# Forty-eight more turns of the identity in TensorE's order, at three places of the second half

## The reference

```python
x = x + tanh(g_xattn[0]) * L0_xattn(ctx, layernorm(x))     # 8 heads of 64, keys = context and tokens, 589 keys
x = x + tanh(g_ffn[0])   * L0_ffn(layernorm(x))            # quantised weights and rows, conv over 3 tokens, silu
x = x + tanh(g_xattn[1]) * L1_xattn(layernorm(x), ctx, ctx)# 16 heads of 8, rotary, 77 keys
x = x + tanh(g_ffn[1])   * L1_ffn(layernorm(x))            # 8 experts, the best 2 per token, and a shared one
```

## Time and profile before

| | us |
|---|---|
| median of 3 runs | 272.95 |
| lowest, highest | 271.57, 273.73 |
| the profiled execution, its own time | 269.39 |
| its span, first to last instruction | 267.6 |
| busy in the span: PE, DVE, ACT, POOL | 255.1, 223.9, 190.8, 32.2 |
| mean granted clock of PE, share of full speed | 0.98 |

### The profile page before, as it was taken

The page is one execution under the profiler, slowest core; times in us unless marked ns, Lnnn a source line. Parts: engine busy times, 40 slices in busy tenths (PEclk is TensorE's granted clock), DMA queues, the critical chain, the costliest instruction groups (busy, mean ns, idle before and its releaser), DMA issues.

```text
span 267.6 us, 5491 instructions
## 1 busy us (share of the span) xinstructions
PE 255.1 (95%) x1782; PEld 188.7 (71%) x1782; DVE 223.9 (84%) x551; ACT 190.8 (71%) x474; POOL 32.2 (12%) x57
## 2 busy tenths in 40 slices
PE   7899999999999999999999999979989798999996
PEld 3567778777788876787778887758756554566675
DVE  6599988967578769999996889999999898698861
ACT  1578868786668787698997954577997888645551
POOL 3000101100101001000000112400021201242330
PEclk9999999999999999999999999999999796899999
DMA  6292392301200034003000000000000000000001
GB/s 187 56 246 76 79 312 69 90 2 25 67 1 4 0 90 92 0 0 80 15 2 0 2 0 2 1 1 2 0 1 2 2 2 0 0 2 21 10 13 39
DMA packets 8850, 10.71 MB, mean 40 GB/s; under 512 B 1116, under 2 KB 5878, under 8 KB 8822
## 3 DMA queue, kind: packets, MB, share of 16 engines
q1 hardware_dynamic: 7792, 9.70, 13.5%
q10 hardware_dynamic: 1029, 0.65, 0.8%
HBM read 4.99 MB, written 0.52 MB: 21 GB/s over the span
## 4 chain that ended last, share of the span: by engine, by line
PE 77%; DVE 14%; issue 4%; ACT 4%; DVEq 0%; ACTq 0%
PE slot L532 22%; PE slot L621 13%; PE slot L602 6%; PE slot L603 6%; PE slot L713 3%; PE slot L762 3%; PE slot L696 3%; PE slot L756 3%; PE slot L583 2%; PE slot L768 2%; PE slot L628 2%; PE slot L577 2%; ACT S L923 2%; PE slot L681 2%; PE slot L592 1%
## 5 line engine op out<-in xcount | busy, mean ns | idle before, releaser
L845 ACT ACTIVATE PR<-slot,nm 128x589 f32<-128x589 f32 x64 | 47.7, 750 | 11.5 <-DVE nm L1071 11.0
L1071 DVE TENSOR_REDUCE nm<-slot 128x1 f32<-128x589 f32 x64 | 46.9, 764 | 7.4 <-PE slot L603 6.9
L532 PE MATMUL slot<-K,PR 128*128 128x128 f32 (+1 forms) x320 | 44.7, 277 | 0.5 <-ACT PR L845 0.3
L532 PEld LDWEIGHTS slot<-K,PR 128*128 128x128 f32 (+1 forms) x320 | 35.9, 142 | 11.3 <-issue 5.5
L602 PE MATMUL slot<-KH,Q 128*128 128x296 f32 (+1 forms) x128 | 41.1, 337 | 0.2 <-DVE KL L1065 0.2
L621 PE MATMUL slot<-PT,V 128*64 128x256 f32 (+1 forms) x320 | 38.1, 384 | 0.0
L603 PE MATMUL slot<-KL,Q 128*128 128x296 f32 (+1 forms) x128 | 36.2, 299 | 0.0
L780 ACT ACTIVATE PT<-slot 128x640 f32<-128x640 f32 x45 | 30.7, 704 | 6.4 <-PE slot L532 6.1
L621 PEld LDWEIGHTS slot<-PT,V 128*64 128x64 f32 (+1 forms) x320 | 21.6, 137 | 11.9 <-issue 2.7
L602 PEld LDWEIGHTS slot<-KH,Q 128*128 128x128 f32 x128 | 24.2, 189 | 2.6 <-DVE PT L782 0.7
L603 PEld LDWEIGHTS slot<-KL,Q 128*128 128x128 f32 x128 | 24.2, 189 | 0.7 <-issue 0.5
(11 more groups left out here) (174 smaller groups left out, 510.4 us busy)
## 6 DMA issues: line engine op xcount, KB each, us to landing
KH<-KH SPq DMA_DIRECT2D x16, 147.5 KB, 2.5
KL<-KL SPq DMA_DIRECT2D x16, 147.5 KB, 2.6
CTT<-in_ctxT SPq DMA_DIRECT2D x1, 640.0 KB, 4.9
K<-in_const SPq DMA_DIRECT2D x1, 589.0 KB, 5.7
WGU<-in_wgu SPq DMA_DIRECT2D x1, 580.0 KB, 6.7
out<-X SPq DMA_DIRECT2D x8, 64.0 KB, 1.5
L1W<-in_l1w SPq DMA_DIRECT2D x1, 384.0 KB, 3.6
WD<-in_wdT SPq DMA_DIRECT2D x1, 320.0 KB, 7.3
```

Of the source, the lines that this page charges most:

```text
L532: return pe.transpose(dst, src, ident[0:p, 0:p])
L845: act.activation(PR[:, s, :], W[:, K0:K0 + KEYS0], ACT.Exp, bias=nm0[:, s:s + 1], accum_out=sum0[:, b, p * 2 + f, t, e:e + 1]).then_inc(pr ...
L1071: dve.tensor_reduce(nm0[:, s:s + 1], W[:, K0:K0 + KEYS0], AX.X, ALU.max, negate=True).then_inc(max_ready, 1)
```

## The change

Three words of `PLAN` get turns; nothing else is touched. The plan is read as before, so the bank's former holder follows from the order.

```diff
-... a4:D3 f2:F2 f2:A1 a2:D1 f2:F3 ...
+... a4:D3 f2:F2+17@3 f2:A1 a2:D1 f2:F3 ...
-... a4:D1 f4:D3 a1:F7 a1:P1 a6:D2 a4:A1 a1:A1
+... a4:D1 f4:D3 a1:F7+17@6 a1:P1 a6:D2 a4:A1 a1:A1
-... a4:A1 a6:P1 a4:B a4:Ca a4:B a6:D2 ...
+... a4:A1 a6:P1 a4:B+14@1 a4:Ca a4:B a6:D2 ...
```

More of the change, by code:

```diff
@@ L125 @@
 w:F2 w:A1 f4:D3 n:P2 a3:F0 n:D3 w:D1 o:F2 a3:D1 o:D1 o:F5 a4:F2 o:D1 a4:D1 a4:A1 a4:B a4:F0 a4:Ca a4:A1 a1:F7 a1:A1 n:P2 a4:B+8@4 a4:D1
-a4:F6 n:D3 a2:F5 f1:F4 a4:A1 a4:D1 f1:A1 a4:Ca f1:D1 a4:D3 f2:F2 f2:A1 a2:D1 f2:F3 f2:A1 f2:D1 a4:B a4:Ca f2:A2 f2:D1 f2:F5+3@4 f2:D2 f2:F2+7@4 f2:A1
+a4:F6 n:D3 a2:F5 f1:F4 a4:A1 a4:D1 f1:A1 a4:Ca f1:D1 a4:D3 f2:F2+17@3 f2:A1 a2:D1 f2:F3 f2:A1 f2:D1 a4:B a4:Ca f2:A2 f2:D1 f2:F5+3@4 f2:D2 f2:F2+7@4 f2:A1
 a4:A1 f2:A1 f2:D1 f2:A2 a4:F4+26@0 a4:B f2:D2 f2:D1 f2:A2 a4:Ca a4:F6+8@0 a4:D1 f2:A2 f2:D2 a3:P1 a4:A1 f2:D2 a1:P1 a4:D1 f3:F2 f3:D1 f3:F1+2@0 f3:F3 a4:A1
@@ L129 @@
 f3:A1 a1:P1 f4:A1 f4:D2 f4:P2 a4:D1 f4:B+6@1 a1:P1 a6:D0 f4:D3 a4:F4 a6:P1 f3:Ca a4:A1 f4:F7 a1:F1 f4:D2 a6:F6 a4:D1 a1:A1 a2:F0 a4:D3 a4:B a6:A1
-a6:D1 f4:A1 a4:A1 f4:B a4:B a4:Ca a2:D1 f4:D2 a4:F2 a4:D1 a4:F0 f4:P2 a4:Ca a4:A1 a4:D3 a6:B a4:F4 a4:D1 f4:D3 a1:F7 a1:P1 a6:D2 a4:A1 a1:A1
+a6:D1 f4:A1 a4:A1 f4:B a4:B a4:Ca a2:D1 f4:D2 a4:F2 a4:D1 a4:F0 f4:P2 a4:Ca a4:A1 a4:D3 a6:B a4:F4 a4:D1 f4:D3 a1:F7+17@6 a1:P1 a6:D2 a4:A1 a1:A1
 a4:B a4:Ca a4:D1 a4:B a6:D0 a4:Ca a4:F6 a2:F2 a4:D3 a4:D1 a6:P1 a4:A1 a6:P2 a6:F1 a4:B a6:D3 a4:A1 a4:B a6:A1 m1:F0 a4:Ca m1:A1 a2:D1 a4:D3
-a6:D1 a4:F4 a4:F2 m3:F0 a4:D1 a4:Ca a4:D1 a6:B a6:D0 a4:F6 a4:A1 a4:A1 a6:P1 a4:B a4:Ca a4:B a6:D2 m3:D1 a4:Ca m3:A1 a4:D1 a4:A1 a4:F4 m3:D2
+a6:D1 a4:F4 a4:F2 m3:F0 a4:D1 a4:Ca a4:D1 a6:B a6:D0 a4:F6 a4:A1 a4:A1 a6:P1 a4:B+14@1 a4:Ca a4:B a6:D2 m3:D1 a4:Ca m3:A1 a4:D1 a4:A1 a4:F4 m3:D2
 a6:F2 a6:P2 a6:A1 m2:F0 a4:D1 a6:D1 m2:A1 a6:D3 a4:B m2:B a4:A1 m1:F3 a4:D3 a4:Ca a4:D3 m2:A2 a6:B a4:B a6:D0 m2:F6 m2:P1 m2:D1 a4:Ca m2:B
```

## The result

The changed kernel takes 273.39 us, the median of 20 runs, against 271.84 us of the kernel before in the same runs: a ratio of 1.0059, 95% interval 1.003 to 1.0088. It is 1.6 us slower. The forecast was 0.6 us slower with a range of 270.4 to 277.2; the time lies in it, and the direction was right. The profiled execution took 272.25 us with a span of 270.5, where the one before had 269.39 and 267.6: 2.9 us more. The two figures differ because executions of one and the same kernel differ in how long PE's clock is down, and because the ten products with which PE starts (L768) take 6.0 us in one trace and 7.6 in another. The profiled execution before had a mean clock of 0.980; in the 57 executions of the kernel before that were timed beside the experiments the mean was 0.973 (0.961 to 0.987), in 19 of the changed kernel 0.989 (a twentieth, of 294.1 us at 0.844, is left out of this mean).

The account below looks back on a forecast made before the run. PE was taken as busy nearly everywhere, with DVE setting the pace from 176 to 209.7 us and half-speed stretches after PE's idle gaps. 1.06 + 2.2 - 2.6 = +0.6 us on 272.95 gave 273.6 us, range 270.4 to 277.2.

Parts of the forecast that it names:

- the sum of +0.6: Whole kernel: 1.06 + 2.2 - 2.6 us over the three places, carried onto 272.95 to give 273.6 us.
- First place: 17 turns in bank 3 ahead of `f2`: PE 1.32 us late, DVE starts 1.06 us late; cost 1.06 us.
- hangs on what PE does around a gap: Argument that the clock fell behind the second gap but not the equally long first; for full clock at both places.
- faster rival: Timed runs lose two more half-speed stretches, one behind the first place: -2.8 us, 270.1 us; chance 0.12.
- Second place: 17 turns in bank 6 ahead of `a1`: PE idle until L1270 ends, then turns; cost 2.2 us, ends 0.97 and 3.9.
- in this trace the clock is 0.50 until 212.5: Second place: 1.19 us worth of full-speed work from 210.13 to 212.5, turns end at 213.2; cost 2.2 us.
- Third place: 14 turns in bank 1 ahead of `a4`: 0.56 us late, but full clock behind them; gain 2.6 us.
- that cover is enough: Third place: PE waits 0.4 us for ACT's L930, but three other words precede `m1`'s turns; supports the 2.6 us gain.
- the 3.56 us: Timed runs' excess over the profiled 269.39 us, carried over; guessed as more half-speed stretches, two with 1.7 us each.
- slower rival: Clock falls behind the third place in spite of the turns: +4.3 us, 277.2 us; chance 0.28.
- Full clock at both places: Rival: PE keeps full clock at second and third places, second costing 0.97: -0.6 us, 272.4 us; chance 0.15.

Follow-up runs that it names:

- kernel with one turn: Kernel before with only one turn in bank 6 at the second place, in place of seventeen: 273.93 us, ratio 1.0113.
- the fitted kernel: Kernel before plus 4 turns in bank 3, 17 in bank 7, 4 in bank 1 at the three places: 266.61 and 266.31 us, ratios 0.9839 and 0.9833.

## Why the prediction was right, and which terms were off

The time lay in the range and the direction held, but two of the three terms were off, and that the forecast of 273.6 us came within 0.2 of the 273.39 measured is luck: the sum of +0.6 was 1.0 us too low against the timed runs (2.3 too low against the traces), and the base, the median of three runs at 272.95, lay 1.1 us above the 271.84 of twenty. One reading of the rows was off without weight: below full speed are three of the slices between 207 and 234 us, not four.

**First place: right in mechanism and size.** Forecast 1.06 us of delay of DVE; measured 1.12 in the changed kernel (1.23 at L1122 less the 0.11 of lag) and 1.1 in the kernel with this edit alone. What I did not see is that the clock falls behind this gap in other executions. I had inferred from one trace that it "hangs on what PE does around a gap"; but in the kernel with the third place alone all is unchanged up to here and the clock in 176 to 189 us is 0.87, where it was 1.00. There the gap costs 1.3 us: L681 behind the 26 turns stands at 188.04, less 1.45 us of start lag 186.59, against 185.28 before. Seventeen turns spare this in some executions and cost 1.1 in all; four spare it and cost nothing. This was part of my faster rival, which the one trace spoke against; it exists, but is worth only 1.3 us in some executions, not 3.4.

**Second place: right in mechanism, undersized.** Forecast 2.2 us with ends of 0.97 and 3.9; measured 3.93 - 1.22 = 2.7. PE waited for L1270 as forecast, 0.57 us longer than before (2.45 against 1.88). The step that was off is "in this trace the clock is 0.50 until 212.5": the sum left the half-speed stretch where it had been, so that most of it fell on idle time and on turns that nobody waits for. It came some 3 us later, from about 212.4 us on. The seventeen turns took 2.48 us up to the work behind them, where they took 1.95 at full clock in bank 7, and the real work from there to L681 took 2.51 in place of 1.52. The kernel with one turn shows that the seventeen turns aren't needed for the cost.

**Third place: the term that was off most.** Forecast a gain of 2.6 us if the clock holds; it held, and the gain was 3.93 - 2.87 = 1.06. The time from the start of L681 ahead of the place to the start of L751 behind it tells the two parts of this term apart:

| kernel | turns at the third place | clock behind it | L681 to L751, us |
|---|---|---|---|
| before | none | 0.50 | 11.92 |
| 17 in bank 7 at the second place alone | none | 1.00 | 9.87 |
| 4 at the third place alone, and the fitted kernel | 4 | 1.00 | 9.87 |
| changed | 14 | 1.00 | 10.86 |

So fourteen turns delay by 0.99 us, where the sum had 0.56: the turns of `S` start 1.05 us late (226.69 less 3.93 is 222.76, before 221.71), and L681 behind them then waits 0.25 us for ACT's copy L794, a wait that the prediction didn't have. And full clock gives back only 2.05 us, where the sum had 3.17, half of the half-speed stretch. This larger part is lost even where no turn delays anything.

The failed step is "that cover is enough". I set only ACT's L930 against PE, and not DVE's L1008 behind it. Five turns of `S` behind L713 PE is still 1.98 us ahead of its former course in the changed kernel (231.67 less 3.93, against 229.72), and 2.98 where nothing is delayed (7.32 us from L681, against 10.30). Two words later it waits 0.64 us for the rows `XN` that L1008 normalises, in every one of these traces with full clock. The lines of the kernel with 17 turns in bank 7 alone:
```profile
220.06 0.79 PE L681 MATMUL slot<-KBD,Q 32*128 32x308 f32 x4
...
227.38 0.71 PE L532 MATMUL slot<-K,S 128*128 128x128 f32 x5
...
228.30 1.40 DVE L1008 TENSOR_SCALAR XN<-X,mvx,vex 128x128 f32<-128x128 f32 x2
228.32 1.04 POOL L520 TENSOR_TENSOR HM<-HM,cwt 128x512 f32<-128x512 f32 x1 [4.79 <-ACT HM L946]
...
229.59 0.50 PE L532 MATMUL slot<-K,XN 128*128 128x128 f32 x2 [0.64 <-ACT PT L794]
229.93 0.61 PE L751 MATMUL slot<-L1W,A1T 128*128 128x128 f32 x4
```

The profile names L794 as the releaser here. But the turns read what L1008 writes, and they begin 0.14 us after the first of the two L1008 ends, which took 1.15 us; before, at 209.55, that distance was 0.14 as well. In the changed kernel it is the same, by the line's least, median and greatest duration in ns and POOL's timeline:
```profile
L1008 DVE TENSOR_SCALAR XN<-X,mvx,vex x2: 332/762/1191, 232.5 to 233.7; 128x128 f32<-128x128 f32 x2
```
```profile
232.61 1.04 POOL L520 TENSOR_TENSOR HM<-HM,cwt 128x512 f32<-128x512 f32 x1 [5.78 <-ACT HM L946]
```
The first L1008 took 1.19 us (232.54 to 233.73), POOL's L520 ran from 232.61 to 233.65. At its usual 0.34 it would have ended at 232.88, before PE was done with L756 at 233.24: by this estimate the wait wouldn't exist. In all eight traces with full clock behind the third place one L1008 takes 1.15 to 1.20 us beside L520; in the five with half speed there L520 starts after it, and none takes more than 0.35. So a faster PE brings L520 forward onto L1008. The trace of before had shown the same twice:
```profile
199.30 0.72 POOL L506 TENSOR_TENSOR X<-X,BO 128x256 f32<-128x256 f32 x1
199.43 1.01 DVE L1008 TENSOR_SCALAR XN<-X,mvx,vex 128x128 f32<-128x128 f32 x2
...
234.15 1.04 POOL L520 TENSOR_TENSOR HM<-HM,cwt 128x512 f32<-128x512 f32 x1 [1.29 <-ACT HM L946]
234.21 1.00 DVE L1005 TENSOR_SCALAR vex<-mvx 128x2 f32<-128x2 f32 x1
```
The first of the two L1008 took 0.68 us, twice its usual time, and L1005 1.00 us in place of 0.17; both ended within 0.1 us of POOL's instruction. Not every step of POOL does this: beside its L481, at 6 us, L1008 took its 0.34. This fits the Trainium skill, page "GPSIMD Engine Reference", section "Specifications", by which GpSimd shares its SBUF interfaces with VectorE and contends with some of its instructions; no run here took POOL's step away to prove it.

**The sum.** 1.12 + 2.7 - 1.06 + 0.11 = 2.87 us, the difference of the spans of the profiles (270.5 - 267.6). The forecast of +0.6 was low by the third term (1.5) and the second (0.5). The timed runs show only +1.6, since the trace of before was one of its better executions (mean clock 0.980, where 57 average 0.973): others had more half-speed time to lose. The prediction's guess for the 3.56 us, more half-speed time in the timed runs, holds in part: 1.1 us of it was the base of three runs.

**The clock.** The Trainium skill's rule that transposes don't count ("TensorE: Matmul & The Clock Gate", "Part 4: PE-mode transpose") would have made the slower rival true. The runs contradict it: 25 added turns in the fitted kernel take the mean clock from 0.973 to 0.999 and more, in all twelve executions. The slower rival falls. Full clock at both places did not occur with bank 6, and occurs with bank 7 (mean 0.9997).

Open: why four turns are enough at the third place, and why the clock falls behind a gap in one execution and not in the next. In the kernel with bank 7 alone the clock stayed full behind the third gap without any turn there. The executions differ by up to 1.6 us in their start; whether that decides is not shown.

## What to carry to other kernels

A filler that writes somewhere needs a place that is free when the gap opens, not when it closes: look up what releases the buffer before counting how many fillers fit, and count from that release to the moment when the real work is due. A wait put ahead of a filler can cost more than the filler, since it prolongs the idle time that the filler was to shorten. When one engine gets faster, redo the cover through every engine behind it, and look at which instructions of two other engines now come to run side by side. One trace of a kernel whose clock differs between executions tells one course out of several: compare at equal mean clock.

## What the runs showed of the hardware that I had not expected

- Behind one and the same 1.9 us gap the clock fell in some executions and not in others (0.87 and 1.00 in 176 to 189 us, with the same program up to there). The mean clocks of the kernel before go from 0.961 to 0.987, and its times over 4.9 us (269.47 to 274.37).
- One turn behind a prolonged wait left PE at half speed for 10.2 us, seventeen turns there for 3.4 (profiles of the two kernels, one execution each); the mean clocks over all executions are 0.961 and 0.972.
- A DVE `TENSOR_SCALAR` that began within 0.15 us of POOL's L520 or L506, both `TENSOR_TENSOR` of 256 or 512 columns, ended within 0.1 us of it, whatever its own length: 128x128 took 1.19 us in place of 0.34, 128x2 1.00 in place of 0.17.
